# Experts stage of a two-layer perceiver kernel: the down projection's last 64 rows as two one-pass products instead of one fp32 product

## The chip, the core and the metric

The kernel runs on one core of one Trainium2 chip. The metric is the device time of one execution in microseconds (us). The kernel before takes 2097.53 us, the median of 3 runs (2090.31 to 2100.91).

## The reference, cut to what matters

The whole program is six residual steps (latent attention, self-attention and a feed-forward, twice). The change lies in the last one, a mixture of 32 experts over 1024 tokens of width 512. Each token keeps at most 8 experts (top-k of a softmax, pruned where a share is below 0.05), and then

```python
def expert_step(acc, xs):
    w_gu, w_d, c_e = xs                 # (384, 512), (512, 192), (1024,)
    gu = x @ w_gu.T
    g, u = jnp.split(gu, 2, axis=-1)    # 192 columns each
    h = jax.nn.silu(g) * u
    acc = acc + h @ w_d.T * c_e[:, None]
    return (acc, None)
```

The down projection `h @ w_d.T` contracts over 192 hidden values, 128 and a rest of 64.

## The kernel before, in words

The last stage (class `Experts`, tiles named `L1f_...`) gathers each expert's tokens into blocks of 128 rows. There are 95 blocks, a worst case fixed at build time; those past the real ones work on spare rows. For a block j

- GpSimd (POOL) fetches 128 token rows with an indirect DMA (`L1f_xg`), five blocks ahead; TensorE turns them (L2670) and ScalarE (ACT) keeps them (`L1f_xT`, L2765);
- TensorE makes gate and up values with four fp32 products of 128x384 against the expert's weights (`hidden`, recorded at L99 with `L1f_w`, two records to a product, as every fp32 product here);
- ACT applies silu (L2718), VectorE (DVE) multiplies by the up half and the token's share (`L1f_z`, L2785), TensorE turns z (L2687 for the first 128 columns, L2688 for the other 64), ACT keeps both in `L1f_zT` (L2726, L2727);
- TensorE multiplies by the down weights with two fp32 products of 128x512 (`down`, L2695 and L2696). The second has only 64 real rows; its other 64 are zeros on both sides, which two memsets on POOL put into `L1f_zT` once and which the host laid out in the weights;
- DVE copies the result to SBUF (`L1f_y`, L2793), and POOL adds it into a table in DRAM with an indirect DMA (L2967). Two tables take turns, so the add of block j waits for that of block j - 2, and three `L1f_y` buffers take turns.

Every engine runs a fixed program. TensorE's loop body is: `hidden(j)`, `turn_rows(j+1)`, for the first 31 blocks `lay_limits(j+5)` (two one-pass 128x512 products, L2660), `down(j-1)`, `turn_hidden(j)`. ACT's is: silu, `L1f_xT` of j+1, `see(j+5)` (a pass over 1024 counts, L2759, which finds the rows of block j+5), the two copies to `L1f_zT`. DVE's is: three small ops for the share, z, four small ops for the row numbers of j+5 (L2824 to L2829, which wait for `see`), the copy of y of j-1. From block 36 on the counts of `see` come from DRAM (`L1f_laid`, 512 KB each, asked for by SyncE two blocks ahead), and SyncE also reloads expert weights (1280 KB a load) into 6 slots, five blocks ahead, when a block begins a new expert. Weights are addressed by a slot number that each engine loads into a register from SBUF (`value_load`; on TensorE at L2589, on SyncE at L2489).

"fp32r" below is the dtype of values that TensorE multiplies in a single pass; other stages split an fp32 value into such a high part and a low part (value minus high part).

Of the kernel before, what the change touches and what calls it, by code (L numbers as in the profile page):

```python
# [7 lines left out]
ALU = mybir.AluOpType  # L8
ACT = mybir.ActivationFunctionType
F32 = mybir.dt.float32  # L10
F32R = mybir.dt.float32r
# [3 lines left out]
P = 128  # L15
BANK = 512
B, S, D = 32, 32, 512
# [15 lines left out]
E2 = EI - P  # L33
# [2284 lines left out]
class Experts(Stage):  # L2318
# [18 lines left out]
    def __init__(self, sh, name, number, left, arena, out, left_early):  # L2337
# [46 lines left out]
        self.zT = [sb(f"zT{i}", [P, 2, P]) for i in range(2)]  # L2384
# [22 lines left out]
        self.rest_clear, self.early_clear = take("down_mixed", 2), take("hx_hi", 2)  # L2407
# [8 lines left out]
    def adds(self, t):  # L2416

        return len(range(t, self.LAST, 2))

# [263 lines left out]
    def turn_hidden(self, pe, j):  # L2683
        pe.wait_ge(self.z_made, j + 1)
        pe.wait_ge(self.zT_set, 2 * j)
        z = self.z[j % 2]
        pe.e.transpose(self.z_bank()[:, 0:P], z[:, 0:P], self.sh.ident[:])  # L2687
        pe.e.transpose(self.z_bank()[0:E2, P:2 * P], z[:, P:EI], self.sh.ident[:]).then_inc(self.z_turned.sem, 1)  # L2688

    def down(self, pe, j, slot):  # L2690
        pe.wait_ge(self.rest_clear, 2)
        pe.wait_ge(self.zT_set, 2 * j + 2)
        pe.wait_ge(self.y_set, j - 1)
        zT, out, at = self.zT[j % 2], self.y_bank(j), self.GU + D
        pe.e.matmul(out, zT[:, 0, :], self.weights(slot, self.GU, at), start=True, stop=False)  # L2695
        pe.e.matmul(out, zT[:, 1, :], self.weights(slot, at, at + D), start=False, stop=True).then_inc(self.y_made.sem, 1)  # L2696
# [3 lines left out]
    def scalar(self, act):  # L2700
# [12 lines left out]
        self.keep_rows(act, 0)  # L2713
        act.e.copy(self.tri[0:NE, :], self.upto[0:NE, :]).then_inc(self.counts_set.sem, 1)
        for j in range(self.BLOCKS):
            act.wait_ge(self.hidden_made, j + 1)
            act.wait_ge(self.z_made, j - 1)
            act.e.activation(self.sg[j % 2][:], self.gu_bank(j)[:, 0:EI], ACT.Silu).then_inc(self.gated.sem, 1)  # L2718
            if j + 1 < self.BLOCKS:
                self.keep_rows(act, j + 1)  # L2720
            if j + self.AHEAD < self.BLOCKS:
                self.see(act, j + self.AHEAD)
            act.wait_ge(self.z_turned, j + 1)
            act.wait_ge(self.y_made, j - 1)
            act.wait_ge(self.rest_clear, 2)
            act.e.copy(self.zT[j % 2][:, 0, :], self.z_bank()[:, 0:P]).then_inc(self.zT_set.sem, 1)  # L2726
            act.e.copy(self.zT[j % 2][0:E2, 1, :], self.z_bank()[0:E2, P:2 * P]).then_inc(self.zT_set.sem, 1)  # L2727
        act.wait_ge(self.y_made, self.BLOCKS)
        act.e.copy(self.last_parts()[0], self.y_bank(self.LAST)).then_inc(self.last_hi.sem, 1)
        self.store(act)  # L2730

# [37 lines left out]
    def vector(self, dve):  # L2769
# [10 lines left out]
        for j in range(self.BLOCKS + 1):  # L2780
# [6 lines left out]
            if j + self.AHEAD < self.BLOCKS:  # L2787
                self.find_row(dve, j + self.AHEAD)
            if 0 < j < self.BLOCKS:
                y = j - 1  # L2790
                dve.wait_ge(self.y_made, y + 1)
                self.y_left(dve, y - self.NY)
                dve.e.tensor_copy(self.y[y % self.NY][:], self.y_bank(y)).then_inc(self.y_set.sem, 1)  # L2793
            if j == self.LAST - 2:
                self.find_goal(dve)
# [7 lines left out]
        for i in range(NT):  # L2803
            dve.wait_ge(self.odd_back[i // 2], 16)
            dve.wait_ge(self.last_added, i + 1)
            dve.e.tensor_tensor(sh.x[:, i, :], sh.x[:, i, :], self.h[:, i, :], ALU.add).then_inc(self.both.sem, 1)

# [143 lines left out]
    def gpsimd(self, pool):  # L2951
        self.begin(pool)
        for zT in self.zT:
            pool.e.memset(zT[:, 1, :], 0.0).then_inc(self.rest_clear.sem, 1)
# [138 lines left out]
def layout(i):  # L3093
# [73 lines left out]
    for e in range(NE):  # L3167
# [3 lines left out]
        experts[e, 0:E2, at + D:] = dn[e, P:EI, :]  # L3171
# [22 lines left out]
```

## Time and profile before

| | |
|---|---|
| median of 3 runs | 2097.53 us |
| the profiled execution | 2095.59 us, span of its instructions 2093.8 us |
| busy, share of the span | PE 1973.9 us (94%), PE's weight loads 69%, DVE 58%, POOL 48%, ACT 41% |
| the blocks of the experts stage | from 1578.4 us to about 2074 us of the span |
| TensorE's mean granted clock | 0.983 of full speed |

"PE" is TensorE's multiplying, "PEld" its loading of weights, which overlaps it; "PEldq" and "SPq" are what the sequencers of TensorE and SyncE do. A record's duration is longer than its share of the engine where records overlap, so work that runs back to back is priced by the distance between starts. The DMA share of a stretch is the mean busy share of 16 engines.

### The profile page before, as it was taken

How to read it: one execution, taken by the hardware profiler on the slowest of the kernel's cores; microseconds unless marked ns; L12 is line 12 of the kernel's file. 1: busy time of each engine (PE TensorE's matmuls, PEld its weight loads, DVE VectorE, ACT ScalarE, POOL GpSimd, SP SyncE). 2: the span in 40 equal slices, each digit the busy share in tenths (PEclk: the TensorE clock that was granted, in tenths of full speed). 3: DMA queues.
4: the chain of work that ended last, by engine and by line, in shares of the span. 5: the costliest groups of instructions: out<-in, count | busy, mean ns of one | idle time of the engine just before them, and what ended most of it. 6: DMA issues, size and time to landing. Idle time of an engine off the chain costs nothing. (4 is left out here: it accounts for less than half of the span.)

```text
span 2093.8 us, 29249 instructions
## 1 busy us (share of the span) xinstructions
PE 1973.9 (94%) x9274; PEld 1435.7 (69%) x9274; DVE 1212.1 (58%) x2691; ACT 867.5 (41%) x2163; POOL 1004.0 (48%) x928
## 2 busy tenths in 40 slices
PE   7989999999999999999987999989979999999996
PEld 6857998886588744666655899977755555555553
DVE  4578787467551122677766788678863433444444
ACT  2555555233322100344445555435515444545451
POOL 1248885211352100577678788486204444555552
PEclk9999999999999999999999999999988999999998
DMA  4552332200311100122143233110336999898886
GB/s 182 201 192 64 98 97 65 82 1 1 121 41 55 35 0 0 42 92 92 52 145 106 74 99 109 66 68 1 121 139 191 310 296 313 210 220 209 220 210 181
DMA packets 104949, 251.47 MB, mean 120 GB/s; under 512 B 14801, under 2 KB 40913, under 8 KB 96305
## 3 DMA queue, kind: packets, MB, share of 16 engines
q1 hardware_dynamic: 82224, 196.02, 27.7%
q0 software_dynamic: 21136, 51.11, 11.8%
q10 hardware_dynamic: 1440, 2.49, 0.3%
q8 instruction: 78, 1.28, 0.2%
q14 instruction: 71, 0.57, 0.1%
HBM read 279.44 MB, written 55.07 MB: 160 GB/s over the span
## 5 line engine op out<-in xcount | busy, mean ns | idle before, releaser
L99 PE MATMUL banks<-L1f_w,L1f_xT 128*128 x760 | 265.0, 492 | 2.6 <-issue 1.7
L2967 POOL DMA_INDIRECT moe_sums<-L1f_y,L1f_row x94 | 149.3, 1588 | 220.0 <-DVE L1f_is_who L2834 167.2
L99 PEld LDWEIGHTS banks<-L1f_w,L1f_xT 128*128 128x128 f32 x760 | 138.0, 192 | 82.4 <-issue 7.3
L160 POOL TENSOR_TENSOR rstd<-rstd,power 128x1 f32<-128x1 f32 x48 | 32.0, 666 | 221.4 <-DVE rstd L154 221.4
L2785 DVE SCALAR_TENSOR_TENSOR L1f_z<-banks,L1f_share,L1f_sg 128x192 f32<-128x192 f32 x95 | 39.7, 418 | 147.4 <-ACT L1f_sg L2718 147.4
L2975 POOL DMA_INDIRECT L1f_xg<-moe_rows,L1f_row x95 | 94.1, 991 | 61.5 <-DVE L1f_spare L2825 24.7
L2718 ACT ACTIVATE L1f_sg<-banks 128x192 f32<-128x192 f32 x95 | 31.4, 331 | 205.2 <-PE banks L99 205.2
L99 PE MATMUL banks<-L0f_down,L0f_z 128*128 128x512 f32 x256 | 111.1, 592 | 1.5 <-DVE L0f_z L2242 1.5
L99 PE MATMUL banks<-L0f_hT_hi,L0f_ug_hi 128*128 128x512 f32 x256 | 100.0, 391 | 0.0
L99 PE MATMUL banks<-L0f_hT_lo,L0f_ug_hi 128*128 128x512 f32 x256 | 99.6, 389 | 0.0
L99 PE MATMUL banks<-L0f_hT_hi,L0f_ug_lo 128*128 128x512 f32 x256 | 99.6, 389 | 0.0
L2695 PE MATMUL banks<-L1f_w,L1f_zT 128*128 x190 | 97.4, 594 | 1.5 <-ACT L1f_zT L2727 1.5
L2314 POOL TENSOR_TENSOR L0f_ug_lo<-w,L0f_ug_hi 128x512 fp32r<-128x512 f32 x32 | 42.9, 1353 | 113.1 <-ACT L0f_ug_hi L2218 113.1
L2696 PE MATMUL banks<-L1f_w,L1f_zT 128*128 x190 | 97.0, 592 | 0.0
L1208 PE MATMUL banks<-L1x_y,L1x_u 128*128 128x512 f32 x192 | 87.8, 593 | 6.0 <-DVE L1x_away_next L363 2.4
L99 PE MATMUL banks<-L1x_wn_hi,L1x_q 128*128 128x512 f32 x256 | 91.7, 420 | 0.0
L625 ACT ACTIVATE L0x_prob<-banks,L0x_small 128x256 f32<-128x256 f32 x128 | 58.9, 473 | 79.1 <-DVE L0x_small L688 79.1
L99 PE MATMUL banks<-L0x_wn_hi,L0x_q 128*128 128x512 f32 x256 | 91.7, 420 | 0.0
L625 ACT ACTIVATE L1x_prob<-banks,L1x_small 128x256 f32<-128x256 f32 x128 | 58.9, 473 | 78.9 <-DVE L1x_small L688 78.9
L2824 DVE TENSOR_SCALAR L1f_row_f<-L1f_found 128x1 f32<-128x1 f32 x95 | 14.6, 154 | 129.6 <-ACT L1f_sign L2759 129.5
L99 PEld LDWEIGHTS banks<-L0f_down,L0f_z 128*128 128x128 f32 x256 | 48.1, 190 | 59.7 <-issue 59.7
L2242 DVE SCALAR_TENSOR_TENSOR L0f_z<-banks,L0f_su,L0f_sg 128x1024 f32<-128x1024 f32 x16 | 20.5, 1283 | 109.7 <-PE banks L99 109.7
(433 smaller groups left out, 5726.9 us busy)
## 6 DMA issues: line engine op xcount, KB each, us to landing
L1f_w<-in_experts SPq DMA_DIRECT2D x95, 1280.0 KB
L1f_laid<-moe_counts SPq DMA_DIRECT2D x59, 512.0 KB, 5.4
w<-in_L1x_heads SPq DMA_DIRECT2D x16, 704.0 KB, 4.2
L0x_q<-L0x_far SPq DMA_DIRECT2D x20, 512.0 KB
L1x_q<-L1x_far SPq DMA_DIRECT2D x20, 512.0 KB
w<-in_L0x_heads SPq DMA_DIRECT2D x8, 1216.0 KB, 6.3
L0x_far<-L0x_away_far SPq DMA_DIRECT2D x8, 1024.0 KB
w<-in_wug SPq DMA_DIRECT2D x8, 1024.0 KB, 4.9
```

What stands on the lines that cost most here:

```text
L99: ins = pe.e.matmul(out, w, m, start=first and n == 0, stop=last and n == len(pairs) - 1)
L160: pool.e.tensor_tensor(self.rstd[:, i:i + 1], self.rstd[:, i:i + 1], self.power[:, 0:1], ALU.pow).then_inc(self.rstd_set.sem, 1)
L625: act.e.activation(dst[:, r, :], bank[:, (r % 2) * 256:(r % 2 + 1) * 256], ACT.Exp, bias=neg[:, r:r + 1], accum_out=sums[:, r:r + 1]).then ...
L1208: ins = pe.e.matmul(self.sh.psum(self.SMALL), self.u[h % 2][:, c, :], self.y[k % 3][:, c, :], start=c == 0, stop=c == QC - 1)
L2242: dve.e.scalar_tensor_tensor(out=self.z[:, a, :], in0=self.unit(2 * a + 1), scalar=self.su[:, a:a + 1], in1=self.sg[a % 2][:], op0=ALU.mul ...
L2314: pool.e.tensor_tensor(lo[:], self.ug_source(n), hi[:], ALU.subtract).then_inc(self.ug_lo.sem, 1)
L2695: pe.e.matmul(out, zT[:, 0, :], self.weights(slot, self.GU, at), start=True, stop=False)
L2696: pe.e.matmul(out, zT[:, 1, :], self.weights(slot, at, at + D), start=False, stop=True).then_inc(self.y_made.sem, 1)
L2718: act.e.activation(self.sg[j % 2][:], self.gu_bank(j)[:, 0:EI], ACT.Silu).then_inc(self.gated.sem, 1)
L2785: dve.e.scalar_tensor_tensor(out=self.z[j % 2][:], in0=self.gu_bank(j)[:, EI:2 * EI], scalar=self.share[:, j:j + 1], in1=self.sg[j % 2][:] ...
L2967: pool.e.indirect_dma_start(self.sums[j % 2][:, :], bass.IndirectOffsetOnAxis(ap=self.row[:, j:j + 1], axis=0), self.y[j % self.NY][:], No ...
L2975: pool.e.indirect_dma_start(self.xg[j % self.NX][:], None, self.rows_of[:, :], bass.IndirectOffsetOnAxis(ap=self.row[:, j:j + 1], axis=0)) ...
```

## The change

The last 64 rows of the down projection are no longer one fp32 product. Both sides are split into an fp32r high and low part in every block. z's rest is stacked: high part in rows 0 to 63, low part in rows 64 to 127 of a new tile `L1f_z_rest`. The host now lays the weights' last 64 rows out twice, in rows 0 to 63 and again in 64 to 127; ACT makes their high part (128x512) and DVE their low part, each in tiles that are idle by then (`tri_r` for even blocks, `member` for odd ones). Two one-pass 128x512 products, z_rest by the high part and z_rest by the low part, then give (z_hi + z_lo) (w_hi + w_lo).

```diff
+    def rest_parts(self, j):
+        both = self.member[:].rearrange("p i n -> p (i n)") if j % 2 else self.tri_r[:]
+        return both[:, 0:D], both[:, D:2 * D]
...
     def turn_hidden(self, pe, j):
         pe.wait_ge(self.z_made, j + 1)
         pe.wait_ge(self.zT_set, 2 * j)
+        pe.wait_ge(self.z_rest_lo, j)
...
     def down(self, pe, j, slot):
-        pe.wait_ge(self.rest_clear, 2)
         pe.wait_ge(self.zT_set, 2 * j + 2)
+        pe.wait_ge(self.z_rest_lo, j + 1)
+        pe.wait_ge(self.w_rest_hi, j + 1)
+        pe.wait_ge(self.w_rest_lo, j + 1)
         pe.wait_ge(self.y_set, j - 1)
-        zT, out, at = self.zT[j % 2], self.y_bank(j), self.GU + D
-        pe.e.matmul(out, zT[:, 0, :], self.weights(slot, self.GU, at), start=True, stop=False)
-        pe.e.matmul(out, zT[:, 1, :], self.weights(slot, at, at + D), start=False, stop=True).then_inc(self.y_made.sem, 1)
+        out, rest = self.y_bank(j), self.z_rest[j % 2][:]
+        pe.e.matmul(out, self.zT[j % 2][:], self.weights(slot, self.GU, self.GU + D), start=True, stop=False)
+        accumulate(pe, out, [(rest, part) for part in self.rest_parts(j)], first=False).then_inc(self.y_made.sem, 1)
...
         for j in range(self.BLOCKS):
+            self.rest_high(act, j)
             act.wait_ge(self.hidden_made, j + 1)
...
+    def rest_high(self, act, j):
+        slot = act.e.value_load(self.slot_i[0:1, j:j + 1], min_val=0, max_val=self.NW - 1)
+        act.wait_ge(self.w_in[j % self.NW], 16 * (j // self.NW + 1))
+        act.wait_ge(self.y_made, j - 1)
+        at = self.GU + D
+        act.e.copy(self.rest_parts(j)[0], self.weights(slot, at, at + D)).then_inc(self.w_rest_hi.sem, 1)
...
                 self.find_row(dve, j + self.AHEAD)
+            if j < self.BLOCKS:
+                self.rest_low(dve, j)
             if 0 < j < self.BLOCKS:
...
                 dve.e.tensor_copy(self.y[y % self.NY][:], self.y_bank(y)).then_inc(self.y_set.sem, 1)
+            if j < self.BLOCKS:
+                self.z_rest_low(dve, j)
...
+    def rest_low(self, dve, j):
+        hi, lo = self.rest_parts(j)
+        slot = dve.e.value_load(self.slot_i[0:1, j:j + 1], min_val=0, max_val=self.NW - 1)
+        dve.wait_ge(self.w_rest_hi, j + 1)
+        at = self.GU + D
+        dve.e.tensor_tensor(lo, self.weights(slot, at, at + D), hi, ALU.subtract).then_inc(self.w_rest_lo.sem, 1)
+
+    def z_rest_low(self, dve, j):
+        rest = self.z_rest[j % 2]
+        dve.wait_ge(self.zT_set, 2 * j + 2)
+        dve.e.tensor_tensor(rest[E2:P, :], self.z_bank()[0:E2, P:2 * P], rest[0:E2, :],
+                            ALU.subtract).then_inc(self.z_rest_lo.sem, 1)
...
     def gpsimd(self, pool):
         self.begin(pool)
-        for zT in self.zT:
-            pool.e.memset(zT[:, 1, :], 0.0).then_inc(self.rest_clear.sem, 1)
...
-        experts[e, 0:E2, at + D:] = dn[e, P:EI, :]
+        experts[e, 0:E2, at + D:] = experts[e, E2:, at + D:] = dn[e, P:EI, :]
```

On TensorE, in a late block (after `lay_limits` has ended), this stood between two `hidden`s before; L2670 turns the next rows, L2695 and L2696 are `down`, L2687 and L2688 `turn_hidden`, and the register load belongs to the next `hidden`:

```order
L2670 MATMUL banks<-ident,L1f_xg 128x128 x3
L2695 ISA [waits s_ctx_set,s_pT_hi]
L2695 MATMUL banks<-L1f_w,L1f_zT 128x512
L2696 ISA
L2696 MATMUL banks<-L1f_w,L1f_zT 128x512
L2687 MATMUL banks<-ident,L1f_z 128x128 [waits s_z_set]
L2688 MATMUL banks<-ident,L1f_z 64x128
L2589 TENSOR_LOAD L1f_slot_i
```

and this stands there now:

```order
L2676 MATMUL banks<-ident,L1f_xg 128x128 x3
L2704 ISA [waits s_norm_sum,s_wn_set,s_ctx_set,s_copied,s_pT_hi]
L2704 MATMUL banks<-L1f_w,L1f_zT 128x512
L99 MATMUL banks<-L1f_member,L1f_z_rest 128x512 x2
L2694 MATMUL banks<-ident,L1f_z 128x128 [waits s_z_set]
L2695 MATMUL banks<-ident,L1f_z 64x128
L2595 TENSOR_LOAD L1f_slot_i
```

The second product of `down` has become two products on fp32r operands, and the first waits for three more signals (s_wn_set: the weights' high part, s_norm_sum: their low part, s_copied: z's low part). Nothing else moved on TensorE.

On DVE, in the same place of the program, from the last op that finds a row to the next z, before (s_mixed is `down` done, s_added the y buffer free, s_gated silu done):

```order
L2829 CAST L1f_row<-L1f_row_f 128x1 [waits s_row_set]
L2793 COPY L1f_y<-banks 128x512 [waits s_added0,s_mixed]
L2834 TENSOR_SCALAR L1f_is_who<-L1f_iota,L1f_who 128x32 [waits s_rows_landed1]
L2836 TENSOR_TENSOR L1f_picked<-L1f_is_who,L1f_xg 128x32 [waits s_weighed]
L2838 TENSOR_REDUCE L1f_share<-L1f_picked 128x1 [waits s_weighed]
L2785 SCALAR_TENSOR_TENSOR L1f_z<-banks,L1f_share,L1f_sg 128x192 [waits s_prob_turned,s_gated,s_weighed]
```

and now (s_pT_hi is ACT's copies of the turned z done):

```order
L2866 CAST L1f_row<-L1f_row_f 128x1 [waits s_row_set]
L2833 TENSOR_LOAD L1f_slot_i
L2833 ISA x2
L2836 ISA [waits s_wn_set]
L2836 TENSOR_TENSOR L1f_member<-L1f_w,L1f_member 128x512
L2813 COPY L1f_y<-banks 128x512 [waits s_added1,s_mixed]
L2842 TENSOR_TENSOR L1f_z_rest<-banks,L1f_z_rest 64x128 [waits s_pT_hi]
L2871 TENSOR_SCALAR L1f_is_who<-L1f_iota,L1f_who 128x32 [waits s_rows_landed4]
L2873 TENSOR_TENSOR L1f_picked<-L1f_is_who,L1f_xg 128x32 [waits s_weighed]
L2875 TENSOR_REDUCE L1f_share<-L1f_picked 128x1 [waits s_weighed]
L2803 SCALAR_TENSOR_TENSOR L1f_z<-banks,L1f_share,L1f_sg 128x192 [waits s_prob_turned,s_gated,s_weighed]
```

A register load with its address work and a subtraction over 128x512 stand ahead of the y copy, and a small subtraction behind it; the next z comes after all of them.

On ACT, the end of a block and the start of the next, now:

```order
L2736 COPY L1f_zT<-banks 128x128 [waits s_prob_turned]
L2737 CAST L1f_z_rest<-banks 64x128
L2744 TENSOR_LOAD L1f_slot_i
L2744 ISA x2
L2748 ISA [waits s_mixed,s_expert_landed0]
L2748 COPY L1f_tri_r<-L1f_w 128x512
L2729 ACTIVATE L1f_sg<-banks 128x192 [waits s_z_set,s_ug_made]
```

Before, silu (now L2729) followed the two copies of z directly; a register load and a 128x512 cast stand between them now.

## Rows read from the trace of the kernel before

**Rows 1.** Stretches: length, busy per engine (records), granted clock, DMA share, GB/s.

```profile
1640.00:1750.00 110.00, 110.00 (x407) 65.25 (x406) 44.25 (x185) 49.27 (x122) 51.53 (x40) 1.00 0.97 299
1750.00:1780.00 30.00, 28.24 (x100) 15.43 (x99) 11.16 (x46) 13.06 (x33) 14.98 (x12) 1.00 0.99 326
1970.00:2020.00 50.00, 50.00 (x182) 28.45 (x181) 21.49 (x90) 24.95 (x61) 25.98 (x21) 1.00 0.89 215
```

**Rows 2.** Waits from 1580 us on: who waited for whom, total us, times, longest.

```profile
ACT L1f_sg L2718 <- PE banks L99: 205.2, 93, 3.5
```

**Rows 3.** Timeline of PE: start, us, line, operation; starts of `hidden` for blocks 1 and 31.

```profile
1585.69 2.84 PE L99 MATMUL banks<-L1f_w,L1f_xT 128*128 x8 [0.43 <-issue]
...
1748.39 2.75 PE L99 MATMUL banks<-L1f_w,L1f_xT 128*128 x8
```

**Rows 4.** Timeline of one late block, from its `hidden` to the next block's z.

```profile
1901.11 2.75 PE L99 MATMUL banks<-L1f_w,L1f_xT 128*128 x8
...
1903.89 0.33 ACT L2718 ACTIVATE L1f_sg<-banks 128x192 f32<-128x192 f32 x1 [2.16 <-PE banks L99]
...
1904.13 1.02 PE L2695 MATMUL banks<-L1f_w,L1f_zT 128*128 x2
...
1905.85 0.27 PE L2687 MATMUL banks<-ident,L1f_z 128*128 128x128 f32 x1
...
1905.86 0.19 ACT L2759 ACTIVATION_READ_ACCUMULATOR L1f_sign<-L1f_laid,L1f_limit 128x1 f32 x1
...
1906.07 2.75 PE L99 MATMUL banks<-L1f_w,L1f_xT 128*128 x8
1906.09 0.15 DVE L2824 TENSOR_SCALAR L1f_row_f<-L1f_found 128x1 f32<-128x1 f32 x1 [1.36 <-ACT L1f_sign L2759]
...
1906.43 0.26 ACT L2727 COPY L1f_zT<-banks 64x128 f32<-64x128 f32 x1
...
1906.59 0.15 DVE L2829 CAST L1f_row<-L1f_row_f 128x1 uint32<-128x1 f32 x1
1906.67 0.69 DVE L2793 COPY L1f_y<-banks 128x512 f32<-128x512 f32 x1
1907.28 0.23 DVE L2834 TENSOR_SCALAR L1f_is_who<-L1f_iota,L1f_who 128x32 f32<-128x32 f32 x1
...
1907.77 0.19 DVE L2838 TENSOR_REDUCE L1f_share<-L1f_picked 128x1 f32<-128x32 f32 x1
...
1909.27 0.42 DVE L2785 SCALAR_TENSOR_TENSOR L1f_z<-banks,L1f_share,L1f_sg 128x192 f32<-128x192 f32 x1 [1.31 <-ACT L1f_sg L2718]
```

**Rows 5.** Timeline of PEld in an earlier stage: one-pass 128x512 products back to back.

```profile
700.34 0.19 PEld L99 LDWEIGHTS banks<-L0f_hT_lo,L0f_ug_hi 128*128 128x128 f32 x1
700.57 0.19 PEld L99 LDWEIGHTS banks<-L0f_hT_hi,L0f_ug_lo 128*128 128x128 f32 x1
```

**Rows 6.** Groups by form: subtraction on DVE and cast on ACT, 128x512, both from SBUF.

```profile
L2276 DVE TENSOR_TENSOR L0f_hT_lo<-L0f_sg,L0f_hT_hi 128x512 fp32r<-128x512 f32 x8 | 5.5, 692 | 5.5 <-ACT L0f_hT_hi L2209 5.3
L2218 ACT CAST L0f_ug_hi<-w 128x512 fp32r<-128x512 f32 x32 | 18.1, 615 | 0.0
```

**Rows 7.** Line L2589, TensorE's register load: ns min/median/max, first and last start.

```profile
L2589 PEldq TENSOR_LOAD <-L1f_slot_i x94: 297/382/1146, 1584.8 to 2064.8; - x94
```

**Rows 8.** Timeline of a block whose z came late: z, PE's turns, the next `hidden`.

```profile
1767.75 0.42 DVE L2785 SCALAR_TENSOR_TENSOR L1f_z<-banks,L1f_share,L1f_sg 128x192 f32<-128x192 f32 x1
...
1768.28 0.11 PEld L2688 LDWEIGHTS banks<-ident,L1f_z 128*64 128x64 f32 x1
1769.07 0.30 PEld L99 LDWEIGHTS banks<-L1f_w,L1f_xT 128*128 128x128 f32 x2 [0.68 <-issue]
```

**Rows 9.** DMA issues, 1640 to 1750 us: median us from issue to landing.

```profile
moe_sums<-L1f_y,L1f_row POOLq DMA_INDIRECT x20, 9.6
```

**Rows 10.** Timeline at the end of the weight loads: an add, then a `see`, held by DMAs.

```profile
1751.11 1.59 POOL L2967 DMA_INDIRECT moe_sums<-L1f_y,L1f_row  x1 [4.18 <-DMA moe_sums<-L1f_y,L1f_row]
...
1771.59 1.15 ACT L2759 ACTIVATE L1f_sign<-L1f_laid,L1f_limit 128x1024 f32<-128x1024 f32 x1 [4.52 <-DMA L1f_laid<-moe_counts]
```

More of the change, by code:

```diff
@@ L2383, in __init__ @@
         self.sg, self.z = ([sb(f"{key}{i}", [P, EI]) for i in range(2)] for key in ("sg", "z"))
-        self.zT = [sb(f"zT{i}", [P, 2, P]) for i in range(2)]
+        self.zT, self.z_rest = [sb(f"zT{i}", [P, P]) for i in range(2)], [sb(f"z_rest{i}", [P, P], F32R) for i in range(2)]
         self.y = [sb(f"y{i}", [P, D]) for i in range(self.NY)]
@@ L2406, in __init__ @@
         self.lane_set, self.steps_to = take("ffn_scaled", 1), {}
-        self.rest_clear, self.early_clear = take("down_mixed", 2), take("hx_hi", 2)
+        self.w_rest_hi, self.w_rest_lo, self.z_rest_lo = take("wn_set", n), take("norm_sum", n), take("copied", n)
+        self.early_clear = take("hx_hi", 2)
         self.even_back = [take(f"x_landed{i}", 16) for i in range(NT)]
@@ L2713, in scalar @@
         self.keep_rows(act, 0)
+        act.wait_ge(self.planned, 3)
         act.e.copy(self.tri[0:NE, :], self.upto[0:NE, :]).then_inc(self.counts_set.sem, 1)
         for j in range(self.BLOCKS):
+            self.rest_high(act, j)
             act.wait_ge(self.hidden_made, j + 1)
@@ L2724, in scalar @@
             act.wait_ge(self.y_made, j - 1)
-            act.wait_ge(self.rest_clear, 2)
-            act.e.copy(self.zT[j % 2][:, 0, :], self.z_bank()[:, 0:P]).then_inc(self.zT_set.sem, 1)
-            act.e.copy(self.zT[j % 2][0:E2, 1, :], self.z_bank()[0:E2, P:2 * P]).then_inc(self.zT_set.sem, 1)
+            act.e.copy(self.zT[j % 2][:], self.z_bank()[:, 0:P]).then_inc(self.zT_set.sem, 1)
+            act.e.copy(self.z_rest[j % 2][0:E2, :], self.z_bank()[0:E2, P:2 * P]).then_inc(self.zT_set.sem, 1)
         act.wait_ge(self.y_made, self.BLOCKS)
```

## The prediction

> **What bounds the kernel now.** I read the stretches first, then the waits, then the timeline of single blocks. In the experts stage PE is busy for 110.00 of 110 us and for 50.00 of 50 us, at a granted clock of 1.00, while DVE and ACT are under half busy [rows 1]. The waits say the same: ACT's silu waits for `hidden` 93 times, 205.2 us in all [rows 2], and PE waits for nobody. So a block costs what PE's instructions cost. There are two rhythms. `hidden` of block 1 starts at 1585.69 and that of block 31 at 1748.39, 30 blocks of 5.42 us [rows 3]; a late block, without `lay_limits`, takes 1906.07 - 1901.11 = 4.96 us [rows 4], and there are 63 of those intervals (blocks 31 to 94). The one place where PE is not full is 1750 to 1780 us (28.24 of 30, DMA share 0.99) [rows 1], where a `see` waited 4.52 us for its counts [rows 10].
>
> **What the change takes off PE.** `down` occupies PE from 1904.13 to 1905.85, 1.72 us for two fp32 products, 0.86 each [rows 4]. One-pass products of the same shape start 0.23 us apart (700.34, 700.57) [rows 5], so two cost 0.46. A block saves 0.86 - 0.46 = 0.40 us of PE. Left to PE alone, the rhythms would be 5.02 and 4.56 us. The real question is whether DVE's new work lets PE keep them.
>
> **What it adds.** On ACT, in each block: a register load and a 128x512 cast, 0.62 us [rows 6]. ACT's last copy of z starts 5.32 us after the block's `hidden` [rows 4]; with 0.79 us for the load (below) and 0.62 for the cast it is free at 6.7. The next silu is due 2.78 us into the next block, at 7.3 or later. It is hidden, with 0.6 us to spare.
>
> On DVE I follow one late block, time counted from its `hidden` (1901.11) [rows 4]. The `see` of block j+5 ends on ACT at 4.94; the row ops run from 4.98, and the last, the cast, starts at 5.48. So far nothing moves, since all of it hangs on silu and `see`. Now comes the register load. Its own record is short on PE, 0.30 us at the least, 0.38 at the median [rows 7]; what counts is when the next instruction that uses the register starts. The only place that shows it bare is a block whose z came late: PE's last turn loads at 1768.28, the load follows, and the next `hidden` starts at 1769.07, 0.79 us later [rows 8]. I take this 0.79 for DVE. Then:
> - subtraction over 128x512 starts at 5.48 + 0.79 = 6.27; it takes 0.69 [rows 6], and a 0.69 us op lets the next start after 0.61 (y copy 1906.67, next 1907.28) [rows 4];
> - y copy at 6.88, z's low part at 7.49; between a 32-column op (0.19) and the 192-column z (0.42) [rows 4], 128 columns make about 0.33, so the next starts 0.25 later;
> - the share ops from 7.74; from the first of them to the end of the third is 0.68 [rows 4]; z of the next block starts at 8.44 and ends at 8.86.
>
> Before, that z could start at 8.16 (1909.27), as soon as silu was through, and TensorE needed it only at 4.96 + 4.74 = 9.70. Now PE would want to turn it at 4.56 + 4.34 = 8.90, which is just met. But behind the turn stands the register load of the following `hidden`, and it can be issued only after the turn's wait has passed. Until now it lay under the running `down`. From the end of a late z to the next `hidden` took 1769.07 - 1768.17 = 0.90 us [rows 8]. So the `hidden` two blocks on can't start before 8.86 + 0.90 = 9.76, and two blocks take at least 9.76: a rhythm of **4.88 us**, not 4.56. z's low part is ready at 7.49 + 0.33 = 7.82, and the next `down` starts at 4.88 + 3.02 = 7.90, so that wait costs about nothing. For the first 30 blocks the same bound gives 4.88 or a little less, under PE's own 5.02, so they get their full 0.40.
>
> What bounds the load on DVE: if it hid altogether, the rhythm would be PE's 4.56; with the longest record on PE, 1.15 instead of 0.30 [rows 7], it would be 0.79 + 0.85 = 1.64 us, and the rhythm 4.88 + 0.85/2 = 5.30. I stay by 0.79, the measured case.
>
> A rule of the Trainium skill speaks against the change here: "DMA: Bandwidth & Descriptors", section "Latency and other measured facts", puts the floor of a `tensor_load` at about 600 ns. The trace shows records of 0.30 us at the least, so the rule doesn't hold for this load on PE; no run here shows it on DVE yet. By the rule (an estimate from that page) the load would be 0.30 us dearer, the rhythm 5.03, and the late blocks would gain nothing.
>
> **DMA.** The bytes stay the same, and they have less time. In the first stretch 299 GB/s at 5.42 us a block become 299 x 5.42 / 5.02 = 323, and 326 is the most that a stretch shows [rows 1]. The adds land in 9.6 us at the median [rows 9], and each waits for the one two blocks back, so two blocks can't be much shorter than 9.6; they take 10.04. One add already waited so [rows 10]. Three y buffers give a slack of 3 x 5.02 - 9.6 = 5.5 us before DVE feels it. I therefore expect both to hold, but tightly, and the `see` waits behind the last weight loads to grow: today PE is idle there for 30 - 28.24 = 1.8 us [rows 1], with a `see` held for 4.52 us [rows 10]. The bounds are 0 and all of the first stretch's gain, 12 us; the nearest row is that 1.8, and since PE now comes to the place some blocks' savings earlier, I take 3.
>
> **The rest.** The two memsets on POOL go, two small fills at the stage's start; nothing. Before the first block ACT does one more load and cast (1.4 us) while PE's first `hidden` runs. The last `down` waits for z's low part, 0.3 us, and is 0.40 shorter. All of it comes to 0.
>
> **The sum.** First stretch 30 x 0.40 = 12.0. Late blocks 63 x (4.96 - 4.88) = 5.0. Less 3 for DMA: 14 us. The profiled execution took 2095.6 us, so it becomes 2081.6; that execution lies 1.9 us under the median of the three runs, which themselves spread over 10. I say 2082.
>
> **The rivals.**
> - *PE keeps its rhythm (0.24).* The register load on DVE runs ahead while ACT is waited for or costs half, so late blocks take 4.56 to 4.65. Worth 12 + 63 x 0.36 = 35, less 3: 2063 us. For it: on PE the load is quite hidden in an ordinary block. Against: on DVE it stands behind row ops that wait.
> - *No change (0.20).* The load costs DVE 0.95 us or a little more, so late blocks stay at 4.96 (4.88 + 0.16/2) or above, and DMA takes a good part of the first stretch's 12 us: 2087 to 2097. For it: PE's median record is 0.08 us above the least [rows 7]; DMA share 0.97; 9.6 us against 10.04. The Trainium skill's floor for the load would bring this case about. Against: 326 GB/s was reached with more in the queue.
> - *Slower (0.13).* DVE becomes the bound outright. With the load at its upper bound, 1.64 us, late blocks take 5.30 and cost 63 x 0.34 = 21 us; the first 30 take 5.25 and give 5. 2095.6 + 21 - 5 + 1 = 2113. It decides against the change from about 1.15 us a load on (rhythm 5.06: 63 x 0.10 = 6 lost, against 12 - 3 won, and the first 30 blocks then start to lose too). For it: a load's record on PE reached 1.15 us. Against: the median is a third of that.
> - *It doesn't do what it says (0.03):* the products on `L1f_z_rest` run at the fp32 rate, nothing is saved and DVE's chain stays: 2100.
>
> **How the numbers follow.** My forecast has 0.40, with a range of its own from 2074 to 2087 (load between 0.6 and 0.95 us, DMA between 1 and 6). A measurement of this kernel can't tell less than about 0.5% (10 us) from no change. Faster by more than that, under 2087: 0.40 and 0.24, together with a part of the third case, 0.67. Within 0.5%: 0.19. Slower: 0.14. The range takes in the first rival down to 2060 and the no-change case up to 2098; that leaves about 0.17 outside.
>
> **What would show it.** Right: blocks 1 to 30 start 5.02 us apart and late ones 4.8 to 4.95, with a gap of some 0.3 us on PE ahead of `hidden`, and in the waits z's turn waiting for DVE's z; on DVE 0.7 to 0.8 us idle ahead of the subtraction over `L1f_w`; ACT's silu still waiting for PE. Wrong: late blocks at 4.56 with no gap (the load hides); a gap ahead of `down` instead (z's low part comes last); first blocks above 5.1 us with adds waiting for adds (DMA); products on `L1f_z_rest` 0.4 us apart.

## The result, and the profile after

The changed kernel takes 2102.09 us (median, 2097.09 to 2110.83), the kernel before 2096.11 us in the same series: a ratio of 1.0033, interval 1.0023 to 1.0043. It is slower by 0.3%, 20 us above the 2082 that was forecast and outside the range. The profiled execution took 2102.82 us with a span of 2101.0, against a span of 2093.8 before, at nearly the same mean granted clock (0.981 and 0.983).

The stretches first, as in [rows 1]; the columns are length, busy time of PE, PEld, DVE, ACT and POOL, clock, DMA share, GB/s:

```profile
1640.00:1750.00 110.00, 107.68 (x420) 66.78 (x419) 67.61 (x232) 64.44 (x149) 56.38 (x44) 1.00 0.99 310
1750.00:1780.00 30.00, 25.17 (x92) 14.48 (x91) 15.86 (x55) 15.02 (x35) 13.60 (x11) 1.00 0.97 302
1970.00:2020.00 50.00, 47.98 (x174) 27.64 (x174) 31.04 (x107) 29.34 (x68) 25.01 (x20) 1.00 0.83 207
```

PE, full before, now has gaps in all three. The last row counts 174 records on PE where [rows 1] had 182. A block leaves 18 of them in either kernel, so 9.7 blocks went through 50 us where 10.1 did. The clock is 1.00 in both, so it plays no part. The waits from 1580 us to the end say who is late now:

```profile
POOL moe_sums L3002 <- DVE L1f_y L2813: 144.1, 62, 5.2
ACT L1f_sg L2729 <- PE banks L99: 119.9, 94, 2.0
...
PEld banks L99 <- issue: 70.3, 256, 2.0
...
DVE L1f_member L2836 <- issue: 24.0, 34, 1.2
DVE L1f_tri_r L2836 <- issue: 23.0, 31, 1.3
POOL moe_sums L3002 <- DMA moe_sums<-L1f_y,L1f_row: 22.3, 8, 4.5
...
DVE L1f_tri_r L2836 <- ACT L1f_member L2748: 16.9, 17, 1.6
DVE L1f_z L2803 <- ACT L1f_sg L2729: 14.6, 12, 5.7
DVE L1f_member L2836 <- ACT L1f_tri_r L2748: 14.5, 13, 2.0
...
PE banks L2704 <- DVE L1f_z_rest L2842: 6.2, 4, 1.9
```

ACT's silu waits for PE 119.9 us instead of 205.2 [rows 2]. DVE's z waits for silu only 12 times in 95 blocks: in the others DVE comes to z when silu is through, so DVE sets z. Its two big waits of kind "issue" stand ahead of the subtraction (L2836, into `L1f_member` and `L1f_tri_r` by turns). That is the register load: the engine waits for no other engine, only for its own sequencer. The two rows that name ACT's cast (16.9 and 14.5 us) are the same wait under another name: they name the cast into the other tile, that of the next block, while the cast that the subtraction needs ended at least 2.59 us earlier in every one of the 95 blocks. All four rows make 78.4 us in 95 blocks.

Time per block, from the start of one silu to the next on ACT, for the kernels of this study (worked out from the trace of each; "late" are blocks 41 to 94):

| kernel | blocks 1–31 | 31–41 | late | span |
|---|---|---|---|---|
| before | 5.42 | 5.32 | 4.99 | 2093.8 |
| after | 5.22 | 5.57 | 5.16 | 2101.0 |
| k3: all the work, fp32 product kept | 5.43 | 5.54 | 5.21 | 2109.4 |
| k4: weights split in two blocks only | 5.04 | 5.18 | 4.65 | 2065.6 |
| k1: DVE's load and subtraction behind z | 5.03 | 5.52 | 4.81 | 2077.1 |
| k2: no load on ACT and DVE | 5.16 | 5.29 | 4.67 | 2064.6 |
| k6: DVE's load ahead of z's wait | 5.03 | 5.45 | 5.14 | 2089.3 |
| k9: PE's load ahead of `down` | 5.17 | 5.41 | 4.97 | 2084.2 |
| k10: all three loads ahead | 5.11 | 5.21 | 4.58 | 2058.1 |
| k7: after, late rows not fetched | 5.14 | 5.54 | 5.13 | 2097.7 |
| k8: after, late adds left out | 5.11 | 5.55 | 5.05 | 2082.9 |
| k5: k4 without later weights | 5.16 | 4.74 | 4.59 | 2060.8 |

Each trace is one execution: those of k2 and k8 are their fastest (2066.5 and 2084.8 us, medians 2072.2 and 2088.0), that of k6 is among its slowest (2091.1, median 2085.5). How far two traces of the same instructions differ shows in the first stretch of the changed kernel, k7 and k8, which are alike up to there: 5.22, 5.14 and 5.11.

From before to after the span grew by 7.2 us: -6.0 in the first 30 blocks (30 x 0.20), +2.5 in the next ten, +8.9 in the 53 late ones (53 x 0.168), -0.4 behind the last block, and +2.2 ahead of block 1, where only ACT's first loads and casts are new (over the twelve traces the silu of block 1 starts anywhere from 1586.5 to 1592.0 us, so I draw nothing from it).

`hidden` of block 1 and of block 31, on the timeline of PE, answer to [rows 3]: (1744.65 - 1587.97) / 30 = 5.22.

```profile
1587.97 2.20 PE L99 MATMUL banks<-L1f_w,L1f_xT 128*128 x6 [0.44 <-issue]
...
1744.65 2.75 PE L99 MATMUL banks<-L1f_w,L1f_xT 128*128 x8
```

Two late blocks on the timeline (start, length; rows of PE and DVE, from one `hidden` to the next but one) answer to [rows 4]:

```profile
1940.50 2.84 PE L99 MATMUL banks<-L1f_w,L1f_xT 128*128 x8
...
1945.16 2.80 PE L99 MATMUL banks<-L1f_w,L1f_xT 128*128 x8
...
1945.57 0.15 DVE L2861 TENSOR_SCALAR L1f_row_f<-L1f_found 128x1 f32<-128x1 f32 x1 [1.36 <-ACT L1f_sign L2777]
...
1946.08 0.15 DVE L2866 CAST L1f_row<-L1f_row_f 128x1 uint32<-128x1 f32 x1
...
1946.85 0.69 DVE L2836 TENSOR_TENSOR L1f_tri_r<-L1f_w,L1f_tri_r 128x512 fp32r<-128x512 f32 x1 [0.62 <-issue]
1947.46 0.68 DVE L2813 COPY L1f_y<-banks 128x512 f32<-128x512 f32 x1
...
1948.17 0.28 DVE L2842 TENSOR_TENSOR L1f_z_rest<-banks,L1f_z_rest 64x128 fp32r<-64x128 f32 x1
...
1948.49 0.24 DVE L2871 TENSOR_SCALAR L1f_is_who<-L1f_iota,L1f_who 128x32 f32<-128x32 f32 x1
...
1948.66 1.12 PE L2704 MATMUL banks<-L1f_w,L1f_zT 128*128 x2 [0.26 <-issue]
...
1949.21 0.42 DVE L2803 SCALAR_TENSOR_TENSOR L1f_z<-banks,L1f_share,L1f_sg 128x192 f32<-128x192 f32 x1
...
1950.20 0.27 PE L2695 MATMUL banks<-ident,L1f_z 128*64 128x128 f32 x1
...
1950.54 1.23 PE L99 MATMUL banks<-L1f_w,L1f_xT 128*128 x3
```

The pair shows the chain that the prediction built: row ops, load, subtraction, y copy, z's low part, share ops, z, then PE's turn and its bare load. The blocks take 4.66 and 5.38 us, 10.04 together, where 9.76 were worked out. And this is a pair with a short load. A second path stands close behind the first: `down` (L2704) starts at 1948.66, held by z's low part, which ended at 1948.45, and the turn, which comes after `down`, would have let `hidden` start at about 1950.31 (an estimate from the 0.11 us between the last turn and `hidden` one block earlier, 1945.05 and 1945.16); the bare load makes it 1950.54. Elsewhere the load is longer; the next rows are the same stretch of DVE, 42 us earlier:

```profile
1904.46 0.15 DVE L2866 CAST L1f_row<-L1f_row_f 128x1 uint32<-128x1 f32 x1
...
1905.91 0.69 DVE L2836 TENSOR_TENSOR L1f_tri_r<-L1f_w,L1f_tri_r 128x512 fp32r<-128x512 f32 x1 [1.30 <-issue]
```

From the cast to the subtraction it is 1.45 us here, 0.77 in the pair. The lines of the register loads themselves (count, ns min/median/max, first and last start), late blocks, DVE, ACT and PE:

```profile
L2833 DVEq TENSOR_LOAD <-L1f_slot_i x56: 300/541/1010, 1784.9 to 2067.1; - x56
L2744 ACTq TENSOR_LOAD <-L1f_slot_i x56: 273/474/1027, 1784.6 to 2068.7; - x56
L2595 PEldq TENSOR_LOAD <-L1f_slot_i x55: 295/301/824, 1789.0 to 2067.6; - x55
```

PE's line had 297/382/1146 over all blocks [rows 7]. The same load of four bytes can take 0.30 us or a whole microsecond, and on DVE in this kernel half of them take over 0.54. From the cast to the subtraction it takes the record's length and 0.46 us more, 1.02 us on average in blocks 41 to 88. Over these 48 blocks the four parts of the chain (`hidden` to cast 5.57, cast to subtraction 1.02, subtraction to z 2.40, z to `hidden` 1.33) have a mean sum of 10.32 us for two blocks, which is the rhythm of 5.16.

### The profile page after: what moved, and what is told of

It reads as the page before. It is cut to its first block and busy times, and to the rows that moved or that the text cites. A ratio compares the mean times of both kernels' runs of the same rounds, so it can differ in the third digit from the quotient of the medians.

```text
span 2101.0 us, 30293 instructions
## 1 busy us (share of the span) xinstructions
PE 1964.3 (93%) x9274; PEld 1437.1 (68%) x9274; DVE 1313.0 (62%) x2881; ACT 923.7 (44%) x2258; POOL 1002.8 (48%) x926
## 3 DMA queue, kind: packets, MB, share of 16 engines
q8 instruction: 78, 1.28, 0.2%
## 5 line engine op out<-in xcount | busy, mean ns | idle before, releaser
L99 PE MATMUL banks<-L1f_w,L1f_xT 128*128 x760 | 269.3, 498 | 5.7 <-issue 1.4
L2704 PE MATMUL banks<-L1f_w,L1f_zT 128*128 x190 | 101.7, 617 | 15.3 <-issue 8.5
L2729 ACT ACTIVATE L1f_sg<-banks 128x192 f32<-128x192 f32 x95 | 31.4, 330 | 120.0 <-PE banks L99 119.9
L1310 DVE TENSOR_TENSOR L1x_turn_part<-banks,L1x_sinq 128x512 f32<-128x512 f32 x64 | 41.2, 686 | 62.9 <-PE banks L99 61.0
L1348 POOL TENSOR_TENSOR L1x_y<-L1x_y,L1x_turn_part 128x1024 f32<-128x1024 f32 x32 | 75.5, 2359 | 5.9 <-DVE L1x_y L1320 5.9
L1342 POOL TENSOR_TENSOR xn<-xn,L1x_sinq 128x512 f32<-128x512 f32 x32 | 41.6, 1299 | 75.5 <-ACT xn L1234 75.5
```

The lines of the kernel that those rows point to most:

```text
L99: ins = pe.e.matmul(out, w, m, start=first and n == 0, stop=last and n == len(pairs) - 1)
L1310: dve.e.tensor_tensor(self.by_tile(self.turn_part[k % 2][:, 1 - c, :], 1), self.by_tile(self.wide(k, c), 1), self.table(self.sinq[:, c:c + ...
L1342: pool.e.tensor_tensor(self.by_tile(buf[:], 1), self.by_tile(buf[:], 1), self.table(self.sinq[:, 2:3], 1), ALU.mult).then_inc(self.rest_si ...
L1348: pool.e.tensor_tensor(y[:, 0:2], y[:, 0:2], self.turn_part[k % 2][:], ALU.add).then_inc(self.pair_set.sem, 1)
L2704: pe.e.matmul(out, self.zT[j % 2][:], self.weights(slot, self.GU, self.GU + D), start=True, stop=False)
```

## Experiments

Theory A: DVE's chain, with its register load in the middle, sets the late blocks, and the load is dearer than the 0.79 us assumed. Rival B: DMA takes the gain (the adds, the weight loads). Rival C: the split products save PE less than 0.40 us.

### k3 and k4: the cost alone, the saving alone

k3 does everything that the change adds, but multiplies the last rows in one fp32 product as before:

```diff
-        accumulate(pe, out, [(rest, part) for part in self.rest_parts(j)], first=False).then_inc(self.y_made.sem, 1)
+        at = self.GU + D
+        pe.e.matmul(out, rest.bitcast(F32), self.weights(slot, at, at + D), start=False, stop=True).then_inc(self.y_made.sem, 1)
```

> All of the added work on ACT and DVE with its waits, but no saving on PE: the second product of `down` is one fp32 product again (0.86 us), on the stacked z and the weights' rest laid out twice. Theory: in late blocks PE's 0.40 us saving was worth nothing, so they stay at 5.1 to 5.25 us; the first 30 blocks go back to 5.42 with a few stalls; 2106 to 2116 us. The rival that PE still bounds the late blocks: they go to 5.56, the time to 2135 to 2140 us.

Measured: 2109.99 us, ratio 1.0075 (1.0045 to 1.0104). Late blocks 5.21 us, against 5.16 with PE's saving. In late blocks the 0.40 us that PE saves are worth 0.05: something other than PE's work bounds them. In the first 30 blocks, k3 takes 5.43 and the changed kernel's median block 5.03, so PE's saving is the full 0.40 and rival C falls.

k4 splits the weights in the first two blocks only; later products use these old halves:

```diff
-        pe.wait_ge(self.w_rest_hi, j + 1)
-        pe.wait_ge(self.w_rest_lo, j + 1)
+        pe.wait_ge(self.w_rest_hi, min(j + 1, 2))
+        pe.wait_ge(self.w_rest_lo, min(j + 1, 2))
...
-            self.rest_high(act, j)
+            if j < 2:
+                self.rest_high(act, j)
...
-            if j < self.BLOCKS:
+            if j < 2:
                 self.rest_low(dve, j)
```

> The saving with nearly none of the cost: the weights' rest is split in the first two blocks only and these parts are used by all others (their weights' rest is left out of the result); z's parts are made in every block. Theory: PE bounds every block again, 5.02 us in the first 30 and 4.56 in the late ones, except where DMA holds them: 12 + 25 us less than before, some of it given back to DMA in the first stretch and behind the last weight loads: 2062 to 2070 us. What is missing to 2059 is DMA's share. If DMA bounds the late blocks: 2090 to 2100.

Measured: 2065.92 us, ratio 0.9859 (0.9830 to 0.9888). Blocks of 5.04 and 4.65 us, nearly PE's own 5.02 and 4.56. So the saving is worth 30 us, and splitting the weights in every block costs 36. The 0.08 us that late blocks lack is PE's register load: z ends 3.68 us after its block's `hidden`, PE's load starts 0.05 us later in every block, and the next `hidden` starts 0.95 us after z's end, which makes 4.63 (medians over blocks 42 to 91).

### k1 and k2: the load elsewhere, and no load

k1 moves DVE's load and subtraction in front of the row ops, right behind z, where DVE waits for `see` anyway:

```diff
+                self.rest_low(dve, j)
             if j + self.AHEAD < self.BLOCKS:
                 self.find_row(dve, j + self.AHEAD)
-            if j < self.BLOCKS:
-                self.rest_low(dve, j)
```

> The changed kernel with one step moved: DVE's register load and 128x512 subtraction over the weights' rest stand between z and the row ops, where DVE waits for `see`, instead of between the row ops and the y copy. My theory (late blocks are bound by DVE's chain from `see` over load, subtraction, y copy, z's low part and the share ops to the next z, two blocks per turn of it): the chain loses 0.8 + 0.6 us and falls behind PE, late blocks go from 5.16 us to 4.56 to 4.65, the time to 2060 to 2072 us. The rival that DMA (the adds and the counts) bounds the late blocks: no change, 2100 us. The rival that the register loads themselves hold the other engines (SyncE, PE, ACT) up: 2090 to 2100, since they are all still there.

Measured: 2075.35 us, ratio 0.9891 (0.9856 to 0.9926). The same instructions in another order win 27 us over the changed kernel; the time is 3 us above the theory's range. Late blocks have a median of 4.71 us; the mean is 4.81, because blocks 41 to 48 take 5.1 to 5.5.

k2 takes both new loads away; the cast and the subtraction read a fixed tile instead of the weights:

```diff
-        slot = act.e.value_load(self.slot_i[0:1, j:j + 1], min_val=0, max_val=self.NW - 1)
-        act.e.copy(self.rest_parts(j)[0], self.weights(slot, at, at + D)).then_inc(self.w_rest_hi.sem, 1)
+        act.e.copy(self.rest_parts(j)[0], self.h[:, 0, :]).then_inc(self.w_rest_hi.sem, 1)
...
-        slot = dve.e.value_load(self.slot_i[0:1, j:j + 1], min_val=0, max_val=self.NW - 1)
-        dve.e.tensor_tensor(lo, self.weights(slot, at, at + D), hi, ALU.subtract).then_inc(self.w_rest_lo.sem, 1)
+        dve.e.tensor_tensor(lo, self.h[:, 0, :], hi, ALU.subtract).then_inc(self.w_rest_lo.sem, 1)
```

> The changed kernel without register loads on ACT and DVE: both split a fixed tile of the same size instead of the slot's weights (so the rest of the down weights is left out of the result); the cast and the subtraction stay where they are. Theory: DVE's chain of 10.04 us for two blocks (where its loads are short) loses 0.79 and the long loads' surcharge (0.26 us a block on average), so late blocks take 4.62 to 4.7 and the time is 2064 to 2076 us. If the subtraction and not the load is what hurts, late blocks stay near 4.9 and the time near 2088. DMA as the bound: 2100.

Measured: 2072.15 us, ratio 0.9904 (0.9872 to 0.9936); late blocks 4.67. The cast, the subtraction and z's low part are all still there, in the places of the change. What costs is not this work but the loads in front of it, and of these DVE's: ACT's cast ends in time for silu and for DVE in every block of the changed kernel. That is theory A.

### k7 and k8: what makes a load long

Four bytes from SBUF in 0.3 or in 1.0 us: something must disturb them. Besides the counts (`L1f_laid`), which stay in both experiments, two DMAs run in each late block, the fetch of the next rows (`L1f_xg`) and the adds (`moe_sums`). k7 leaves the fetches out from block 36 on and lets the blocks reuse old rows; k8 leaves the adds out from block 36 on (the waits for them are changed to match, which the cut below leaves out).

```diff
k7:
-            if j + self.AHEAD < self.BLOCKS:
+            if j + self.AHEAD < 36:
k8:
+            if j >= 36:
+                continue
```

> The changed kernel without POOL's fetches from block 36 on (the blocks work on rows left in the six buffers, so the result is not the reference's); the adds, the counts and all else stay. Theory on the long register loads: in late blocks DVE's load has a mean of 0.55 us against 0.30 at the least, since loads made while POOL's fetch and its DMA run are held up. Then without fetches the loads are 0.30 again, late blocks go from 5.16 to 5.02 us, the time to 2092 to 2096. If it is the adds or SyncE's own loads that hold them, the mean stays at 0.5 and the time near 2101.

> The changed kernel without the adds into the DRAM tables from block 36 on (those blocks' results are left out); the fetches stay. If the fetches hold up the register loads: DVE's loads keep a mean above 0.45 in late blocks, which stay above 5.1 us; about 2098 to 2101. If it is the adds: loads at 0.30, late blocks at 5.02, 2092 to 2096.

Measured: k7 2100.08 us, ratio 1.0010 (0.9997 to 1.0022); k8 2087.98 us, ratio 0.9976 (0.9954 to 0.9999). My theory for k7 failed. The time of k8 fell below its 2092 to 2096. DVE's load in late blocks, k7:

```profile
L2834 DVEq TENSOR_LOAD <-L1f_slot_i x56: 300/418/1068, 1788.3 to 2068.5; - x56
```

and k8:

```profile
L2833 DVEq TENSOR_LOAD <-L1f_slot_i x53: 299/303/321, 1788.6 to 2049.8; - x53
```

Without fetches the loads stay long (mean 0.51 us, against 0.55 in the changed kernel); without adds the longest of 53 takes 321 ns, and ACT's and PE's are at their minimum too. So it is the adds that lengthen them. But k8's late blocks still take 5.05 us. Two of its blocks, on the timeline of PE, `hidden` to `hidden`:

```profile
1940.43 2.84 PE L99 MATMUL banks<-L1f_w,L1f_xT 128*128 x8
...
1945.09 2.81 PE L99 MATMUL banks<-L1f_w,L1f_xT 128*128 x8
...
1950.47 1.88 PE L99 MATMUL banks<-L1f_w,L1f_xT 128*128 x5
```

Again 10.04 us for two, in a trace with nothing to disturb the loads. So this is the price of the chain itself, 5.02 a block. (Every eighth block is 0.37 longer: there DVE's address work starts 0.38 us later behind a load that is itself short, 0.31 us. The cause of that is open.) The disturbed loads add 5.161 - 5.045 = 0.12 on top. That fits the chain, which meets one DVE load in two blocks: half of 0.55 - 0.30. Of the 18 us between the two spans the late blocks make 6; the rest lies ahead of block 1, in the first stretch and behind the last block.

### k6, k9, k10: loads issued ahead of the wait

k6 issues DVE's load of the block before DVE waits for silu, when it has just done the share ops, and puts the subtraction behind z as in k1 (that line is left out below):

```diff
+                slot = dve.e.value_load(self.slot_i[0:1, j:j + 1], min_val=0, max_val=self.NW - 1)
...
-    def rest_low(self, dve, j):
+    def rest_low(self, dve, j, slot):
-        slot = dve.e.value_load(self.slot_i[0:1, j:j + 1], min_val=0, max_val=self.NW - 1)
```

> As the kernel with the early subtraction, and DVE's register load yet earlier, after the share ops and before the wait for silu; ACT's and PE's loads stay where they were. Theory: it takes DVE's load out of the way of the row ops, but the slow patches of the kernel with the early subtraction come from PE's bare load (0.8 to 1.0 us when it falls on a fetch), which is still there: 2066 to 2075 us. If DVE's load were the cause: 2062 to 2066.

Measured: 2085.53 us, ratio 0.9936 (0.9913 to 0.9959), ten executions from 2072 to 2093. A miss by at least 10 us, and worse at the median than k1, though DVE has less in its chain. (That loads grow long on a fetch, as the expectation has it, k7 doesn't bear out.) The rows of the loads in late blocks, DVE and PE:

```profile
L2801 DVEq TENSOR_LOAD <-L1f_slot_i x55: 299/304/320, 1788.9 to 2064.8; - x55
L2595 PEldq TENSOR_LOAD <-L1f_slot_i x55: 302/809/1122, 1785.2 to 2062.1; - x55
```

DVE's load is now always short, and PE's has gone from 301 to 809 ns. On the timeline of PE:

```profile
1938.40 0.27 PE L2694 MATMUL banks<-ident,L1f_z 128*128 128x128 f32 x1
...
1938.51 0.27 PE L2695 MATMUL banks<-ident,L1f_z 128*64 128x128 f32 x1
...
1939.17 2.84 PE L99 MATMUL banks<-L1f_w,L1f_xT 128*128 x8 [0.38 <-issue]
```

z ended at 1937.62, 0.78 us before the turn, so DVE isn't late. PE's load starts at 1937.67, as soon as the turn's wait is passed, and takes 0.85 us: it doesn't fit under `down` any more, and `hidden` waits for it. Over blocks 42 to 91 `hidden` starts 1.47 us after z's end here and 0.92 in the changed kernel, with loads of 0.78 and 0.30 us: nearly all of the difference is the load's. Two loads had to get out of the way, not one. k1's bad blocks are of the same kind: in blocks 41 to 47 PE's loads take 0.73 to 1.03 us.

k9 leaves DVE as in the changed kernel and moves only PE's load, that of block j+1 in front of the `down` of block j:

```diff
-                last, slot = slot, pe.e.value_load(self.slot_i[0:1, j:j + 1], min_val=0, max_val=self.NW - 1)
+                last, slot = slot, ahead
+            if j + 1 < self.BLOCKS:
+                ahead = pe.e.value_load(self.slot_i[0:1, j + 1:j + 2], min_val=0, max_val=self.NW - 1)
```

> The changed kernel with PE's register load for the next block ahead of `down` instead of between z's turn and the next `hidden`; the rest as it is. Theory: from the end of a late z to the next `hidden` it takes 0.3 us instead of 0.90, and the wait of `down` for z's low part decides instead (8.16 us after the block's start, 1.54 more to the `hidden` two blocks on: 9.7 for two blocks, plus 0.26 us a turn for long loads on DVE). Late blocks 4.9 to 5.0 us, 2088 to 2093 us. If PE's load plays no part: 5.16 and 2101.

Measured: 2085.04 us, ratio 0.9941 (0.9923 to 0.9959); late blocks 4.97. PE's load out of the way gives 0.19 us a block; the time is 3 us under the range.

k10 is k6 (with its subtraction behind z) and k9 together, and also loads ACT's register one block ahead; the new lines for ACT:

```diff
+        slot = act.e.value_load(self.slot_i[0:1, 0:1], min_val=0, max_val=self.NW - 1)
         for j in range(self.BLOCKS):
-            self.rest_high(act, j)
+            self.rest_high(act, j, slot)
...
+            if j + 1 < self.BLOCKS:
+                slot = act.e.value_load(self.slot_i[0:1, j + 1:j + 2], min_val=0, max_val=self.NW - 1)
             act.wait_ge(self.z_turned, j + 1)
```

> The complete change, with the register loads of all three engines where they wait anyway: DVE's after the share ops and before the wait for silu, its subtraction right behind z, ACT's before the wait for z's turn, PE's ahead of `down`. Theory: nothing of the added work stands on the chain, the first 30 blocks take 5.02 us, late ones 4.56 to 4.65, and what is left is DMA behind the last weight loads: 2058 to 2068 us, at or below the kernel that saves without the cost (2066). Rival: the extra register loads and DMA hold it at the level of the kernel with the early subtraction (2075).

Measured: 2058.12 us (2053.13 to 2060.78), ratio 0.9813 (0.9791 to 0.9834). It computes what both kernels compute and beats both, the changed one by 44 us. The late stretch, then DVE's and PE's loads in late blocks, then three `hidden` and what DVE does between:

```profile
1970.00:2020.00 50.00, 50.00 (x199) 31.06 (x198) 34.47 (x121) 30.77 (x75) 34.41 (x23) 1.00 0.92 216
```

```profile
L2806 DVEq TENSOR_LOAD <-L1f_slot_i x55: 299/303/322, 1787.5 to 2033.8; - x55
L2605 PEldq TENSOR_LOAD <-L1f_slot_i x54: 296/666/1137, 1784.7 to 2027.5; - x54
```

```profile
1931.47 2.75 PE L99 MATMUL banks<-L1f_w,L1f_xT 128*128 x8
...
1932.38 0.15 DVE L2870 CAST L1f_row<-L1f_row_f 128x1 uint32<-128x1 f32 x1
...
1932.46 0.69 DVE L2818 COPY L1f_y<-banks 128x512 f32<-128x512 f32 x1
...
1934.94 0.42 DVE L2809 SCALAR_TENSOR_TENSOR L1f_z<-banks,L1f_share,L1f_sg 128x192 f32<-128x192 f32 x1 [0.75 <-ACT L1f_sg L2733]
...
1936.05 2.75 PE L99 MATMUL banks<-L1f_w,L1f_xT 128*128 x8
...
1940.62 2.75 PE L99 MATMUL banks<-L1f_w,L1f_xT 128*128 x8
```

Blocks of 4.58 and 4.57 us, PE full again, and z waits for silu. PE's loads are still long (median 666 ns, up to 1137), and it costs nothing: they lie under `down`. That is also why k10 beats k4, whose PE still loads behind the turn: 4.58 against 4.65 us a late block.

### k5: the DMA term

k5 is k4 without the weight loads behind the first ones; later blocks multiply by old weights. SyncE's three register loads for each of them go too.

```diff
-            sp.e.dma_start(self.w[:, bass.ds(slot, 1), :].rearrange("p o n -> p (o n)"),
-                           d["experts"][bass.ds(e, 1), :, :].rearrange("o p n -> (o p) n"),
-                           bounds_check="skip_entire_dma", cond=fresh).then_inc(self.w_in[(j + self.NW - 1) % self.NW].sem, 16)
```

> As the kernel with the saving alone, and without the expert weight reloads after the first six loads (the blocks use the six slots' first weights, so the result is not the reference's). It asks what DMA costs: if the weight loads are what holds the blocks 31 to 41 and the adds, these blocks go from 5.18 to 4.62 us, the first 30 stay at 5.02, and the time falls by 5 to 7 us against the kernel with the saving alone, to 2059 to 2061 us. If not, it stays at 2066.

Measured: 2063.20 us, ratio 0.9839 (0.9814 to 0.9863), 2.7 us under k4 and 2 us above the range expected. Blocks 31 to 41 fall from 5.18 to 4.74, 4.4 us in ten blocks; the first 30 rise from 5.04 to 5.16, and there PE's loads have a mean of 0.89 us, long ones with no weights in transit. The weight DMA costs a few us at one place (rival B as far as it goes), and the length of PE's loads does not come from it.

## Why the prediction was wrong

- *PE saves 0.40 us a block: right.* The changed kernel's median block in the first stretch takes 5.03 us (5.02 forecast), the late floor is 4.57 in k10 (4.56 forecast), and k4 gives the whole of it.
- *The late blocks are set by DVE's chain and PE's bare load, over two blocks: right as a mechanism.* (The working's own terms give 8.42 and 9.74 where it has 8.44 and 9.76; I keep its numbers.) In the pair at 1940.50 the terms, forecast and measured, are: cast at 5.48, 5.58 (`hidden` behind a gap runs 2.84 us instead of 2.75, and `see` with it); load 0.79, 0.77; subtraction to y copy 0.61, 0.61; y copy to z's low part 0.61, 0.71; to the share ops 0.25, 0.32; to z 0.70, 0.72; z to `hidden` 1.32 (0.42 and 0.90), 1.33. Sum 9.76 and 10.04.
- *The step that failed* is the sentence "a rhythm of 4.88 us, not 4.56", in two terms. (1) The small ones, each taken at its least or from an operation of another shape, add 0.28 to a pair: 5.02 instead of 4.88, already more than the 4.99 of before. k8 shows this alone. The chain was counted from a `hidden` that doesn't stand behind a gap, while its own result puts one behind a gap. (2) "I stay by 0.79, the measured case" took one bare load on PE for the mean of 95 on DVE. In late blocks DVE's record has a mean of 0.55 us, not 0.30; k8 against the changed kernel prices that at 0.12 us a block. With 0.02 more, from the long eighth blocks less the short last ones, it makes 5.16, so the 53 late blocks lost 8.9 us where 4.2 (53 x 0.08) were to be won.
- *"They get their full 0.40", for the first 30 blocks:* the same step fails here. With a short load the chain takes 9.91 us for two blocks (5.45, 0.77, 2.36 and 1.33), 4.96 a block and not 4.88; PE's own pair takes 10.04. So a load that is 0.13 us too long already costs time. The sum also counted all 63 later intervals at 4.96; the ten from 31 to 41 took 5.32 before.
- *"That wait costs about nothing", for z's low part:* not so. In 31 of the blocks 41 to 88 `down` starts 0.20 us after the low part's end, 3.37 us on average after `hidden` where 3.02 was the forecast. In the changed kernel this path stays just behind PE's load (the pair above), so it adds little to the time. It is why the turn hardly ever waits for z in the waits, a sign that the prediction named.
- *DMA:* I took 3 us. In the first stretch 6 of 12 us are missing (3 to 4 in k7 and k8, which run the same instructions there). They lie in 9 blocks of over 5.3 us. k1 and k6, which move DVE's load and subtraction, have none of these and run at 5.03, although adds wait for adds in k1 as well (26.6 us in 8 waits, 22.3 in the changed kernel). So DVE's chain most likely brings most of it. Blocks 18 and 19 (6.46 and 5.87 us) are of another kind: k10 has such a pair too (6.19, 5.90), k2 also (6.54, 6.96). I did not test that one. Blocks 31 to 41 lost 2.5 us more.
- *"It is hidden, with 0.6 us to spare", for ACT's load: right.* ACT's cast ended before the next silu in all 95 blocks, 1.26 us before it at the median (in the pair above ACT is idle for 0.63 us ahead of silu), and at least 2.59 us before DVE's subtraction.
- *The rivals.* "No change" came nearest: it named a load of 0.95 us or more on DVE, and the mean is 1.02 in blocks 41 to 88. The slower case named 1.15 us as the point of decision, with the time 2113. The result lies between the two. The warning was in [rows 7]: a median of 0.38 and a longest of 1146 ns for a load that needs 0.30. I used the longest as an outer bound and gave nothing for the spread.

In the Trainium skill, "DMA: Bandwidth & Descriptors", section "Latency and other measured facts", a `tensor_load` costs no less than about 600 ns. The records of this case don't bear that out as a floor (k8: 299 to 321 ns on DVE), yet for the late blocks of the changed kernel the figure is nearer to DVE's mean of 0.55 us than my 0.30, and the rhythm worked out from it, 5.03, nearer to the measured 5.16 than 4.88.

## What to carry to other kernels

Before adding a register load to an engine's program, look where it stands: behind a wait that ends late it is bare, and cost here 0.77 us to the next instruction that uses it, or 1.45 at a bad moment. Issue it ahead of the wait, on every engine on the path; k10 wins 44 us by that and by the subtraction's new place, and moving only one of the loads can shift the cost to the other (k6). When the profile names another engine for a wait, check that this engine's work was not done long before (ACT's cast here). When a chain crosses two engines and comes out within 0.1 us of the old rhythm, the small intervals decide: take them from the same chain, with the spread of every record in it, not the least value.

## What I had not expected of the hardware

- A register load from SBUF lasts some 0.30 us at the least, but with the adds' DMAs at work up to 1.28 us on DVE, 1.35 on SP, 1.03 on ACT and 0.95 on PE (all in the changed kernel); with the adds left out, none of 53 on DVE exceeds 321 ns. The fetches of rows do nothing that shows: without them DVE's mean stays at 0.51 us. Why the adds do it (that they read and write back, or the queue they are on) is open.
- The length depends on when in the add the load falls. In the eleven traces with adds, over the register loads of all engines from 1788 us on, 777 of the 1679 that start 1.9 to 3.6 us after the start of the add's issue on POOL take over 0.5 us, and none of the other 1768 does (the longest: 0.47). In k6 PE's loads start 1.97 to 2.73 us after an add's issue and half take over 809 ns; in the changed kernel most start 1.26 us after it and half take 301 or less. A kernel with a fixed rhythm meets the same moment in each block, so that a shift of some tenths of a microsecond on DVE changed a load on PE by half a microsecond.
